# A four-layer network: the first layer's weight, shift and residual add on VectorE, between the steps of its slot, in place of GpSimd

## The reference

```
def _L0_gnn_ref(node_feats, adj_matrix, W_lin, b_lin, W_q, W_k, ln_g, ln_b):
    X, q, k = heads of lrelu(node_feats @ W_lin + b_lin), lrelu(node_feats @ W_q), lrelu(node_feats @ W_k)
    att = sigmoid(q k^T * scale)            # 4 heads, 256 x 256 each
    adj_h = adj * att
    deg = sum(adj_h, axis=-1);  dis = deg ** -0.5
    Y = (dis adj_h dis) X                   # back to [B, N, 128]
    return (Y - mean) * rsqrt(var + eps) * ln_g + ln_b
...
x = x + _L0_gnn_ref(_layernorm(x), adj, ...)
x = x + _L0_ffn_ref(_layernorm(x), ...)
```

## Time and profile before

| | |
|---|---|
| three runs | 958.96, 961.82, 961.0 us; median 961.0 |
| profiled execution | 957.8 us, span 956.0 us |
| busy in the span | PE 695.5 us, DVE 593.8, ACT 431.8, POOL 436.3 |
| mean granted PE clock | 0.856 of full |
| first layer's slots | about 4 to 413 us of the span |
| three adds on GpSimd | x32 each, L801 720 to 802 ns |

### The profile page before, as it was taken

One profiled execution on the slowest core, in us unless ns is written; L12 is line 12 of the kernel. 1 busy time (PEld: TensorE's weight loads), 2 busy tenths in 40 slices (PEclk: granted clock), 3 DMA queues, 4 the chain that ended last, 5 costly groups with the idle time before them and its releaser, 6 DMA issues. The chain is left out here.

```text
span 956.0 us, 18424 instructions
## 1 busy us (share of the span) xinstructions
PE 695.5 (73%) x4886; PEld 543.5 (57%) x4886; DVE 593.8 (62%) x2480; ACT 431.8 (45%) x1018; POOL 436.3 (46%) x478
## 2 busy tenths in 40 slices
PE   3989798888888885405776667676546774699994
PEld 2556565555555553404665556665446673589993
DVE  6898978787878767331333333333267784348898
ACT  4576665565655533103333333332212556567771
POOL 0022245554555557762555555545644310185540
PEclk9998998997898865556889999898768997699998
DMA  7223123222221111822222222222199940102211
GB/s 186 82 63 89 56 78 100 78 80 78 79 78 57 45 35 35 245 87 68 77 77 72 72 83 77 76 72 78 56 216 214 175 110 1 46 1 68 68 36 53
DMA packets 90507, 79.97 MB, mean 84 GB/s; under 512 B 11025, under 2 KB 79810, under 8 KB 89410
## 3 DMA queue, kind: packets, MB, share of 16 engines
q1 hardware_dynamic: 69250, 54.84, 20.5%
q0 software_dynamic: 21184, 24.27, 10.5%
HBM read 46.39 MB, written 32.69 MB: 83 GB/s over the span
## 5 line engine op out<-in xcount | busy, mean ns | idle before, releaser
L1189 POOL DMA_INDIRECT expert_outputs<-y_rows,y_at x144 | 138.5, 962 | 120.8 <-DVE y_rows L1158 77.9
L814 POOL DMA_INDIRECT expert_rows<-rows,row_of x128 | 125.6, 981 | 45.3 <-issue 34.3
L1158 DVE TENSOR_TENSOR y_rows<-psum,f_b 128x256 f32<-128x256 f32 x72 | 30.6, 425 | 124.9 <-PE psum L1042 71.2
L801 POOL TENSOR_TENSOR y_n<-y_n,ln_g 128x256 f32<-128x256 f32 x32 | 23.4, 732 | 185.6 <-ACT y_n L517 185.3
L1092 ACT ACTIVATE hT<-psum,f_b 128x256 f32<-128x256 f32 x144 | 60.5, 471 | 87.6 <-remote 36.7
L1021 PE MATMUL psum<-ident,xin 128*128 128x128 f32 x144 | 33.6, 319 | 90.2 <-DMA xin<-expert_rows 87.8
L1031 PE MATMUL psum<-xinT,wst 128*128 128x256 f32 x288 | 88.2, 434 | 12.1 <-DVE wst L1140 9.9
L1042 PEld LDWEIGHTS psum<-wst,hT 128*128 128x128 f32 x576 | 83.0, 208 | 7.6 <-issue 2.8
L1042 PE MATMUL psum<-wst,hT 128*128 128x128 f32 x576 | 83.2, 292 | 2.5 <-DVE y_rows L1158 2.5
L636 DVE TENSOR_TENSOR adj_h<-psum,adjT 128x1024 f32<-128x1024 f32 x64 | 77.8, 1216 | 9.4 <-ACT psum L476 6.4
L1076 ACT ACTIVATE xinT<-psum 128x256 f32<-128x256 f32 x72 | 27.7, 385 | 116.4 <-PE psum L1021 89.4
(11 more groups left out here) (250 smaller groups left out, 1656.7 us busy)
## 6 DMA issues: line engine op xcount, KB each, us to landing
xin<-expert_rows SPq DMA_DIRECT2D x72, 130.0 KB
adj_in<-in_adj_dram SPq DMA_DIRECT2D x32, 256.0 KB, 3.8
adjT_scratch<-adjT SPq DMA_DIRECT2D x32, 256.0 KB, 3.0
adjT<-adjT_scratch SPq DMA_DIRECT2D x8, 1024.0 KB
xres<-expert_outputs POOLq DMA_DIRECT2D x12, 512.0 KB, 11.3
xres<-in_x_dram SPq DMA_DIRECT2D x16, 256.0 KB, 3.5
out_dram<-yout SPq DMA_DIRECT2D x6, 512.0 KB, 3.1
expert_outputs<-y_rows,y_at POOLq DMA_INDIRECT x144
```

The costliest lines, as they stand in the source:

```text
L814: pool.indirect_dma_start(rows_dram[:, :], bass.IndirectOffsetOnAxis(ap=row_of[:, g % 3, k, t:t + 1], axis=0), rows[:, g % 3, t, :], None) ...
L1189: pool.indirect_dma_start(y_dram[:, :], bass.IndirectOffsetOnAxis(ap=y_at[:, u, r:r + 1], axis=0), y_rows[:, u, r, :], None).then_inc(s_y_ ...
```

## The change

The three operations of `add_attention` are issued by DVE, with the same operands, semaphores and waits, as a generator of three parts. The multiplication comes behind `take_gates`, the addition of `ln_b` behind the next link of the chain, the residual add behind the statistics of x and right ahead of `weigh(s, 0)`. GpSimd keeps `send` alone, with no waits on `s_yn` between the four sends of a slot and those of the next. Line numbers behind the insertion move by 14 on DVE (L685 becomes L699, L679 becomes L693, L709 becomes L723) and by 7 for the sends (L814 becomes L821).

```
+            def add_attention(b):
+                dve.wait_ge(s_yn, b + 1)
+                yn = y_n[:, b % 2, :, :]
+                xb = xres[:, b * TB:(b + 1) * TB, :]
+                nc.vector.tensor_tensor(yn, yn, ln_g[:, :].unsqueeze(1).to_broadcast((P, TB, D)), ALU.mult)\
+                    .then_inc(s_poolc, 1)
+                yield
+                dve.wait_ge(s_poolc, 2 * b + 2)
+                nc.vector.tensor_tensor(yn, yn, ln_b[:, :].unsqueeze(1).to_broadcast((P, TB, D)), ALU.add)\
+                    .then_inc(s_poolc, 1)
+                yield
+                dve.wait_ge(s_poolc, 2 * b + 3)
+                nc.vector.tensor_tensor(xb, yn, xb, ALU.add).then_inc(s_x1, 1)
...
                 if batch(s - 7):
                     take_gates(s - 7)
+                adds = add_attention(s - 4) if batch(s - 4) else iter(())
+                if batch(s - 4) and s == 4:
+                    dve.wait_ge(s_wln, 2 * 16)
+                next(adds, None)
                 next(steps, None)
+                next(adds, None)
                 for t in range(TB):
...
                 if s == NB + 3:
                     centre_weights3(dve)
+                next(adds, None)
                 if batch(s):
                     weigh(s, 0)
...
         def gnn0_gpsimd(pool):
-            pool.wait_ge(s_wln, 2 * 16)
-
-            def add_attention(b):
...
             for s in range(FIRST, LAST + GB):
-                if batch(s - 4):
-                    add_attention(s - 4)
                 g, part = divmod(s - 12, GB)
```

## The result

The changed kernel takes 1030.2 us (median of 4 runs, 1024.0 to 1033.8) where the kernel before takes 961.4 (4 runs, 959.0 to 963.3): ratio 1.071, interval 1.065 to 1.077. The forecast was 944.8 us, range 936 to 955. The sign was wrong, although the effects on VectorE came as forecast.

What follows compares the result with a forecast made beforehand. DVE was taken to end the choosing slots, held there by GpSimd's adds, and something else the ranking slots. Gains of 1.0 + 9.0 + 5.2 + 1.0 = 16.2 us from 961.0 gave 944.8 us, range 936 to 955.

Steps and rivals of the forecast that it cites:

- L728's wait: Layer's end, at 412.08: waits for a rank whose last matmul was recorded long before; 1.0 us gain taken.
- Rival C: Any GpSimd traffic on SBUF holds L717 and L592, so DVE pays 1.06 us per head; 972 us, chance 0.07.
- early slots: Slots at 49.70 to 95.16, without choice steps, DVE ending four: 1.0 us gain, between 0 and 2.6.
- six choosing slots: DVE no longer held by GpSimd's adds at head (0.25 us) and end (1.35 us) of choosing slots: 9.0 us gain.
- six ranking slots: PE's clock stays up, gaining 1.3 us in four of six ranking slots: 5.2 us, between 0 and 7.8.
- a term that I had set to zero: Third slots: L636 already waits for ACT, which covers DVE's added 1.06 us; effect 0.
- rival A: Clock falls in the ranking slots just the same and PE ends them; 952 us, chance 0.22.
- PE's idle time ahead of L315: Ranking slot's head: PE's idle time shrinks from 2.62 to about 1.0 us.
- local forecast of 16.2: Sum of gains: early slots 1.0, choosing slots 9.0, ranking slots 5.2, layer's end 1.0 us.
- The rule that I weighed: DVE can lock GpSimd out of writing descriptor rings, so more DVE work would stretch sends; set aside, median send 0.97 us.

Runs made afterwards that it cites:

- e4: Changed kernel with a GpSimd memset of 128 x 1024 numbers between two sends, in all groups but the last two; 932.7 us (0.971).
- e17: Changed kernel with a memset of 128 x 256 numbers before each send of six groups; 927.5 us (0.968), the kernel before taking 957.5.
- e1: Changed kernel with a GpSimd wait on s_x1 before each slot's 4 sends; 931.9 us against 959.2 of the kernel before (0.973).
- e3: Changed kernel with the s_x1 wait only before every second slot's sends, so 8 sends in a row; 986.1 us (1.029).
- e9: The changed kernel itself, run again; 866.0 us (0.988) where the kernel before took 877.5.
- e12: Kernel before, with a memset of 128 x 256 numbers before each send of six groups; 874.8 us (0.996), the kernel before taking 877.5.
- e13: Changed kernel with a memset of 128 x 256 numbers before each send of six groups; 865.0 us (0.988), the kernel before taking 874.4.
- e18: Changed kernel with a second send of 32 rows, to a spare table, behind each send of 128; 1203.2 us (1.255), the kernel before taking 957.5.
- e16: Changed kernel with a second send of 32 rows, to a spare table, behind each send of 128; 918.1 us (1.046), the kernel before taking 874.4.
- e10: Changed kernel with the s_x1 wait before each slot's 4 sends, as e1; 868.8 us (0.989) where the kernel before took 877.5.
- e7: As e4, plus a memset of 128 x 256 numbers before each of the expert stage's 144 sends; 995.3 us (1.133), the kernel before taking 874.0.

## Why the prediction was wrong

**The step that failed** is the one that I costed at nothing: "GpSimd's 4 sends per slot become 16 in a row: 16 x (0.97 + 0.30) = 20 us, and three of a group's four slots alone last 34.4 us, so they still end before the next group's." I asked whether GpSimd would be late, and it was not: the sends end at 258.6 us, before the slot does. I did not ask what a row of sends does to the other engines' signals. In its place the runs show that the row keeps TensorE's results from ACT and DVE while it lasts: five third slots are 14 us longer each and one later slot 12 (19.2 us), 82 us with the fourth and last slots, and with pauses in the row (e4, e17) or the wait (e1) the lengthening is gone.

**The sign was in the trace before.** I quoted L728's wait as "not explained by rows" and gave it 1 us, between 0 and 6. It stood beside a row of 20 sends, from 383.6 to 408.7 us. ACT's L482 had four waits of the same kind, each in a third slot, where the first four sends of a group run; the second and the third of them in the timeline of before:

```profile
223.33 0.38 ACT L482 ACTIVATE yT<-psum 128x256 f32<-128x256 f32 x1 [2.36 <-remote]
...
270.77 0.38 ACT L482 ACTIVATE yT<-psum 128x256 f32<-128x256 f32 x1 [2.59 <-remote]
```

Such a wait was the only price of a row of sends that the trace had; from it the change's 16 sends in six groups could have been bounded above: the row's 20 us in each, or 120. My range took no such bound.

**Rival C** (slower, held by any traffic of GpSimd) had the right sign and the wrong mechanism: L592 and L731 are not held beside sends (L592 at 239.03 in the changed kernel takes 0.16 us; e3's L731 takes 0.22 to 0.23 in all seven slots in which sends run beside it). Its 972 us rested on VectorE paying 1.06 us per head.

**The terms.** Measured as they were meant, without held signals, by distances between heads of e9 against e12 (the kernel before itself has no trace in the second condition, so its form with short memsets, 0.996 of it, stands in): early slots -1.1 us (forecast 1.0); six choosing slots -9.0 (9.0); six ranking slots -5.2 (5.2, which is luck, next); the slots behind the sixth ranking slot -2.4. Against them stand +4.7 in five third slots, a term that I had set to zero. By the windows of a ranking and a third slot, e12 first, then e9:

```profile
200.70:213.00 12.30, 11.15 (x94) 8.05 (x94) 8.55 (x36) 5.02 (x13) 6.99 (x11) 0.86 0.23 66
213.00:220.80 7.80, 7.67 (x76) 5.14 (x72) 7.20 (x32) 5.29 (x11) 5.16 (x9) 1.00 0.37 106
```

```profile
191.40:203.30 11.90, 10.76 (x86) 8.30 (x90) 9.13 (x38) 6.65 (x14) 0.00 (x0) 0.86 0.15 45
203.30:212.80 9.50, 9.50 (x84) 5.86 (x80) 8.49 (x35) 5.25 (x11) 7.28 (x8) 0.82 0.34 102
```

The clock still falls in the ranking slot, to 0.86 in both, which was rival A. The three ranking slots in which both kernels have 0.86 are only 0.4 us shorter each; the rest of the 5.2 comes from the others, two of which had 0.77 and 0.75 in e12 and have 0.85 and 0.86 in e9. PE's idle time ahead of L315 is 2.28 us in e9, where I had said "near 1". And in e9 the low clock, 1.2 GHz, lasts on into the third slot (0.82) where e12 has 1.00 again. The sum of the distances is 13.2 us, the kernels' ratio 0.988, 11 us: a third of the local forecast of 16.2 did not come, about what the third slots took.

With pacing in the first condition (e1) the kernels' gain is 27 us. By the distances there the ranking slots fall to 10.7 us (12.7 us together instead of 5.2, one of 15.2 us before being 10.5 now), and the third slots to 10.0 (6 us). All distances together give 32 us; the execution profiled was e1's fastest, 924.0 us. Why the clock stays up more in e1's ranking slots (0.94 to 1.00 in four of six) than in e17's (0.81 to 0.82 in four of six) stays open.

**The rule that I weighed** (the Trainium skill, "DMA: Bandwidth & Descriptors", SWDGE vs HWDGE vs iDMA: DVE can lock GpSimd out of writing descriptors) was the wrong one to look at. The page says it of DVE's 2-port mode alone, a condition that the prediction left out, and no run here shows whether the adds use that mode. With the adds on VectorE the 128 sends take 988 ns on average (e9 980, e1 1002), against 981 in the kernel before. The trace shows no stretching to speak of. What went wrong was on the side of those who wait for TensorE, not in GpSimd's own time.

## What to carry to other kernels

When an instruction is moved away from a queue, what it separated moves together: the adds were also the pauses by which GpSimd's sends kept step with the slots. Ask of each queue what the removed work had spaced out, and put the wait back if you take the work. A wait that the profile puts down to nothing on this core is a term without a known price, and gets a bound, not a guess. And compare kernels only within one comparison: the same kernel took 865.0 and 927.5 us on one chip at different times (e13 and e17).

## What the runs showed of the hardware that I had not expected

- Beside rows of GpSimd's indirect DMAs issued 1.27 us apart, ScalarE and VectorE wait for TensorE's results for up to 13.8 us (rows of 16, the line below) and up to 34.6 us (rows of 32, e18, L483 at 570.67); with 0.6 us of pause ahead of each such waits are gone (e17). VectorE's own chain ran on until its next instruction in the list had to read PSUM.

```profile
437.60 0.38 ACT L482 ACTIVATE yT<-psum 128x256 f32<-128x256 f32 x1 [13.75 <-remote]
```

- The effect is there in some comparisons and absent in others, on one chip, for the same kernels (e13 and e17, e16 and e18), and it moves the kernel before by 85 us. What sets the condition, and by which path the signals are held, was not found. The expert stage carries most of the difference between the conditions (242.8 and 185.9 us in e1 and e10), and whether pauses there help in the first condition was not tried; in the second they cost 122 us (e7).
